# Chunked attention inside a fused block: values per chunk pair, keys spread by masks, shifts moved within SBUF, local matmuls over the column tiles in turn

## The reference

```
x + attn(xn) + ffn(xn)
attn(xn) = (chunk16(xn) + chunk16(every third token of xn)) @ Wo.T + bo     # 16 heads of 8
ffn(xn):  y = xn + mla(rmsnorm(xn, w_ln1));  y + moe(rmsnorm(y, w_ln2))
```

## Time and profile before

| | |
|---|---|
| median of 3 runs | 512.22 us (511.31 to 513.36) |
| the profiled execution, its time | 509.05 us |
| its span (first to last instruction) | 507.3 us |
| busy: PE, DVE, ACT, POOL | 405.5, 315.8, 177.9, 76.7 us |
| mean granted TensorE clock | 0.889 |
| DMA packets | 58215, 24.45 MB; 40088 under 512 B |
| waits of SP's queue | 35.6 us on the shifts' way to DRAM (16 times) |

### The profile page before, as it was taken

How to read it: one execution, slowest core, us unless ns; L and a number is a source line. 1 busy time by engine, 2 the same in 40 slices (tenths; PEclk the granted TensorE clock), 3 DMA queues, 4 the chain that set the end, 5 groups by cost and what they waited for, 6 DMA issues and landing times.

```text
span 507.3 us, 11480 instructions
## 1 busy us (share of the span) xinstructions
PE 405.5 (80%) x4288; PEld 245.2 (48%) x4288; DVE 315.8 (62%) x959; ACT 177.9 (35%) x336; POOL 76.7 (15%) x98
## 2 busy tenths in 40 slices
PE   2753259868497988898978786989989998799995
PEld 2331126554364655455646453645634475464552
DVE  6441037655264777568677565585863288888886
ACT  5143102205152454553334344444564322112110
POOL 6065102240102220304202001000010001000000
PEclk9975659979797999899889987898996899999998
DMA  6052642132181332642232145000400000000000
GB/s 207 0 127 53 118 64 64 15 72 36 25 143 31 71 70 36 105 71 43 44 74 29 26 81 79 7 11 9 121 3 2 1 0 1 23 0 21 1 21 23
DMA packets 58215, 24.45 MB, mean 48 GB/s; under 512 B 40088, under 2 KB 55896, under 8 KB 57368
## 3 DMA queue, kind: packets, MB, share of 16 engines
q1 hardware_dynamic: 58160, 23.71, 24.4%
HBM read 12.94 MB, written 8.55 MB: 42 GB/s over the span
## 4 chain that ended last, share of the span: by engine, by line
PE 25%; DVE 21%; issue 20%; SPq 19%; DMA 8%; POOL 4%; ACT 2%; DVEq 0%; POOLq 0%; ACTq 0%
SPq L541 6%; SPq L556 6%; DVE x L1075 6%; DMA shift_dram<-shift 4%; PE bank_c L1205 4%; DVE k_diag L1055 4%; DVE k_diag L1060 3%; SPq L553 3%; PE bank_B L1294 3%; PE bank_B L1110 3%; SPq L567 3%; PE bank_M L1153 2%; DMA q_stack<-in_c_rows 2%; PE bank_M L1263 2%; PE bank_A L1241 2%
## 5 line engine op out<-in xcount | busy, mean ns | idle before, releaser
L805 ACT ACTIVATE p_mla<-bank_B 128x512 f32<-128x512 f32 (+1 forms) x176 | 95.8, 560 | 130.8 <-PE bank_B L1116 129.8
L934 DVE CUSTOM_DVE_ANT_0 differences<-masks,bank_A 128x512 bf16<-128x512 bf16 (+1 forms) x128 | 78.9, 617 | 67.4 <-PE bank_A L1093 59.1
L1110 PE MATMUL bank_B<-q_stack,k_stack 50*128 50x512 bf16 (+3 forms) x256 | 68.7, 325 | 29.7 <-DMA q_stack<-shift_dram 13.6
L1093 PE MATMUL bank_A<-k_stack,q_stack 50*128 50x512 bf16 (+3 forms) x256 | 66.6, 323 | 16.5 <-DMA q_stack<-in_c_rows 13.9
L1294 PE MATMUL bank_B<-xrT,k_diag 128*128 128x512 f32 x128 | 67.3, 631 | 5.7 <-DVE k_diag L1055 4.5
L1110 PEld LDWEIGHTS bank_B<-q_stack,k_stack 50*128 50x128 bf16 x256 | 20.0, 96 | 76.3 <-issue 47.4
L1263 PE MATMUL bank_M<-v_diag,pT_loc 128*32 128x72 f32 x1088 | 50.6, 238 | 4.7 <-DMA v_diag<-v_dram 4.7
L1205 PE MATMUL bank_c<-p_mla,v_mla 128*9 128x128 f32 (+3 forms) x512 | 51.1, 473 | 3.8 <-ACT p_mla L805 3.3
L1116 PE MATMUL bank_B<-masks 64*128 64x64 bf16 (+1 forms) x512 | 53.6, 211 | 0.0
L1263 PEld LDWEIGHTS bank_M<-v_diag,pT_loc 128*32 128x32 f32 x1088 | 47.5, 113 | 7.6 <-issue 6.0
L1116 PEld LDWEIGHTS bank_B<-masks 64*128 64x128 bf16 x512 | 42.2, 100 | 16.2 <-issue 5.2
(11 more groups left out here) (140 smaller groups left out, 531.7 us busy)
## 6 DMA issues: line engine op xcount, KB each, us to landing
parts_dram<-parts SPq DMA_DIRECT2D x16, 192.0 KB, 2.7
k_stack<-parts_dram SPq DMA_DIRECT2D x8, 384.0 KB
q_stack<-parts_dram SPq DMA_DIRECT2D x8, 384.0 KB
parts_dram<-parts SPq DMA_DIRECT2D x16, 128.0 KB, 2.7
k_diag<-k_part SPq DMA_DIRECT2D x32, 34.0 KB
k_diag<-k_part SPq DMA_DIRECT2D x64, 17.0 KB
x<-in_x SPq DMA_DIRECT2D x4, 256.0 KB, 6.4
parts_dram<-parts SPq DMA_DIRECT2D x16, 64.0 KB, 2.3
```

The lines of the kernel that those rows point to most:

```text
L805: drained_by(nc.scalar.activation(p_of(n)[:, m:m + len(heads), 0:w], src, ACT.Exp, scale=SCALE), step)
L934: drained_by(nc.vector.tensor_tensor_reduce(differences[:, 0:w], masked16[:, S - w:], bank[:, 0:w], -1.0, -NEG, ALU.add, ALU.min, dst), step)
L1093: return nc.tensor.matmul(bank_of(step)[:, n * w:(n + 1) * w], q_stack[b % 2][rows, h % 8, i * P:(i + 1) * P], k_stack[b % 2][rows, h % 8, ...
L1110: nc.tensor.matmul(bank_of(step)[:, m * w:(m + 1) * w], k_stack[b % 2][rows, h % 8, j * P:(j + 1) * P], q_stack[b % 2][rows, h % 8, j * P: ...
```

## The change

Local values: LV makes them per chunk pair, on 32 output partitions each, into three banks (68 records in place of 8), ACT copies them between ones already in `v_rows`, one DMA stores them with those ones, and VD is 2 x 8 DMAs per batch in place of 56. Keys: POOL and ACT write `k_diag` as `k_part` times a mask of a head's rows, 4 pieces of 128 x 1088 each; KD's 24 DMAs per batch go. Shifts: two DMAs within SBUF in place of one to DRAM, a wait and one back. Latent output: Y per group of 4 heads once its `bank_c` is copied, YT and X1 behind the last. LS and LO: the innermost loop goes over the four column tiles. The first stack load (ST 0) stands before the local projections of batch 0, waits for each side's parts by itself, and its rows of ones come first of all; the rows of zeros are no longer loaded. Batch 1's projections, which stood ahead of the first scores, are now strewn between them. `SPREAD` has new numbers: KD of batch 2, for one, stands at S unit 76 of 176 (before: 60), MB of side 1 of batch 2 at 79 (52), ST of batch 2 at 86 (73), and batch 2 begins with unit 88. The last LS of a batch and the first of the next stand at units 21 and 54, 75 and 92, 116 and 130.

```diff
-PT_RING = 2
+PT_RING = 1
+KD_PARTS = 4
+OUTPUT_AT = 3
...
-    "scores": [(-0.289, 3.94)],
+    "scores": [(-0.425, 4.13)],
...
+                if back and k == OUTPUT_AT and n > LEAD:
+                    done = groups[n - LEAD - 1]
+                    found.append([("Y",) + done])
+                    if done[1] == GROUP_ORDER[-1]:
+                        found += [[("YT", done[0])], [("X1", done[0])]]
...
-    steps = first[:1] + first[5:6] + [("WF",)] + first[6:] + first[1:5] + [("KD", 0)]
+    lead = [step for step in first if step == ("XT", 0, 1) or step[0] in ("MA", "MB")]
+    steps = first[:1] + lead[:1] + [("WF",)] + lead[1:] + [("ST", 0)]
+    steps += [step for step in first[1:] if step not in lead] + [("KD", 0, n) for n in range(KD_PARTS)]
...
+        v_rows = sb("v_rows", [P, X, QUADS, VX])
+        v_diag = sb("v_diag", [P, X, 8, QUADS - LOCAL_QUADS, VX])
...
# SP
+                    sp.dma_start(v_dram[b], v_rows[:]).then_inc(v_out, 16)
                 if kind == "VD":
...
+                    if step[2]:
+                        wait_full(sp, ("LO", b, LOCAL_UNITS - 1))
+                    elif b:
+                        wait_full(sp, ("LO", b - 1, NLU - 1))
...
+                    for g in range(X):
+                        sp.dma_start(v_diag[CHUNK * g:CHUNK * g + CHUNK, g, :, 0:i1 - i0, :].rearrange("k q i c -> k q (i c)"),
+                                     v_dram[b, :, g, i0:i1, :].rearrange("(q k) i c -> k q (i c)", k=CHUNK)).then_inc(v_diag_in, 16)
-                if kind == "KD":
...
-                    for h in range(H):
-                        rows = slice(HD * h, HD * h + HD)
-                        if h < X:
-                            sp.dma_start(k_diag[rows, :, h, :], k_part[rows, :, :]).then_inc(k_diag_in, 16)
-                        else:
-                            for par in range(2):
-                                sp.dma_start(k_diag[rows, 1 - par, h - X, :],
-                                             k_part[rows, par, :]).then_inc(k_diag_in, 16)
...
                 if kind == "ST":
-                    sp.wait_ge(parts_out, 16 * 6 * 2 * (b + 1))
...
                     for side in range(2):
+                        sp.wait_ge(parts_out[side], 16 * 6 * (b + 1))
...
                 if kind == "SHIFT":
...
-                    sp.dma_start(shift_dram[b, g].rearrange("r p n -> p r n"), shift[:]).then_inc(shift_out, 16)
-                    sp.wait_ge(shift_out, 16 * (n + 1))
...
-                    sp.dma_start(q_stack[b % 2][row:row + 2, a0:a0 + 4, :],
-                                 shift_dram[b, g].rearrange("r (a i) n -> r a (i n)", i=NT)).then_inc(shift_in[g], 16)
+                    for r in range(2):
+                        sp.dma_start(q_stack[b % 2][row + r:row + r + 1, a0:a0 + 4, :].rearrange("o a (i n) -> o (a i) n", n=P),
+                                     shift[:, r, :]).then_inc(shift_in[g], 16)
...
# POOL (k_part is now sorted in 8 copies of 64 partitions in place of 3 of 128)
+                if step[0] == "KD":
+                    _, b, n = step
...
+                    nc.gpsimd.tensor_scalar(k_diag[:, :, n, :], k_part[:], head_mask[:, n:n + 1], None,
+                                            ALU.mult).then_inc(k_diag_by_pool, 1)
...
# ACT
+                elif kind == "KD":
+                    _, b, n = step
+                    if n == 0:
+                        act.wait_ge(heads_in, 16)
+                        act.wait_ge(k_part_ready, b + 1)
+                        if b:
+                            wait_full(act, ("LS", b - 1, NLU - 1))
+                    x = KD_PARTS + n
+                    nc.scalar.activation(k_diag[:, :, x, :], k_part[:], ACT.Copy,
+                                         scale=head_mask[:, x:x + 1]).then_inc(k_diag_by_act, 1)
...
# PE, LS and LO
-                    for n, pair in enumerate(LUNITS[step[2]][0]):
-                        j, c = n % 4, 2 * P * (n // 4)
+                    pairs = LUNITS[step[2]][0]
+                    for t in range(loc_tiles(step)):
                         for a in range(2):
...
+                            for j, pair in enumerate(pairs[4 * t:4 * t + 4]):
...
-                    for n in range(len(LUNITS[step[2]][0])):
-                        i, j = n // 4, n % 4
+                    for i in range(loc_tiles(step)):
                         for g in range(2):
                             c = 2 * w * i + w * g
                             for par in range(2):
...
+                                for j in range(min(4, len(LUNITS[step[2]][0]) - 4 * i)):
```

More of the change, by code:

```diff
@@ L188, in local @@
     def local(b):
-        steps = [("VD", b, 0), ("VD", b, 1)]
+        steps = [("VD", b, 0)]
         for k in range(NLU + 1):
@@ L193, in local @@
             if k == NLU - 1:
-                steps.append(("KD", b + 1) if b + 1 < B else ("WX",))
+                steps += [("KD", b + 1, n) for n in range(KD_PARTS)] if b + 1 < B else [("WX",)]
             if k:
                 steps.append(("LO", b, k - 1))
-                if k + 1 < NLU:
-                    steps.append(("VD", b, k + 1))
+                if k == LOCAL_UNITS:
+                    steps.append(("VD", b, 1))
             if k < NLU:
@@ L226, in plan @@
     lists.append(([("STATS", 0)], *at["statistics"][0]))
-    return steps + merged(*lists)
+    steps += merged(*lists)
+    at = {step: n for n, step in enumerate(steps)}
+    assert all(at["PICK", b] < at["DOWN", b, 1] and at["X1", b] < at["R2", b] for b in range(B))
+    return steps
 def bank_uses(step):
@@ L468, in loc_tiles @@
             return -(-len(LUNITS[step[2]][0]) // 4)
-        def v_dmas(t):
-            return sum(X * len(LUNITS[k % NLU][1]) for k in range(t % 2, t + 1, 2))
         def wait_full(eng, use):
@@ L524, in _ @@
             for step in steps:
                 kind, b = step[0], step[1] if len(step) > 1 else 0
-                if kind == "LV":
-                    wait_drained(sp, step)
-                    sp.dma_start(v_dram[b, 0:S].rearrange("(i p) d -> p i d", p=P), v_nat).then_inc(v_out, 16)
+                if kind == "LV" and step[2] == (QUADS - 1) // 4:
+                    for n in range(step[2] + 1):
+                        wait_drained(sp, ("LV", b, n))
+                    sp.dma_start(v_dram[b], v_rows[:]).then_inc(v_out, 16)
@@ L529, in _ @@
                 if kind == "VD":
[L530 removed]
+                    i0, i1 = SEGMENTS[step[2]]
                     sp.wait_ge(v_out, 16 * (b + 1))
[L532 to L543 removed]
@@ L567, in _ @@
                             sp.dma_start(parts_dram[b, side, hp, t0:t0 + nt].rearrange("t p n -> p t n"),
-                                         src).then_inc(parts_out, 16)
-                if kind == "ST" and b < 2:
-                    for hp in range(2):
-                        row = SLOT * hp + SHIFT_ROW
-                        sp.dma_start(k_stack[b][row:row + 2, :, :],
-                                     rows_dram[0:2, :].rearrange("o (a n) -> o a n", n=S)).then_inc(k_ones_in[b], 16)
+                                         src).then_inc(parts_out[side], 16)
                 if kind == "ST":
-                    sp.wait_ge(parts_out, 16 * 6 * 2 * (b + 1))
                     if b >= 2:
@@ L721, in _ @@
         def _(act):
-            nc.scalar.memzero(late[:, 0:CLEARED]).then_inc(diag_zeroed, 1)
+            nc.scalar.memzero(v_diag[:].rearrange("p x q i c -> p (x q i c)")).then_inc(v_zeroed, 1)
             act.wait_ge(wide_in, 16)
@@ L1227, in _ @@
                 elif kind == "LV":
-                    for i in range(NT):
-                        last = nc.tensor.matmul(bank[:, i * D:(i + 1) * D].rearrange("p (x g d) -> p x g d", x=X, g=2),
-                                                xnT[:, b % 2, i * P:(i + 1) * P],
+                    for pair in range(16 * step[2], min(16 * step[2] + 16, PAIRS)):
+                        first, stp, n = pair_tokens(pair)
+                        j, c = pair % 4, D * (pair // 4 % 4)
+                        last = nc.tensor.matmul(bank[PAIR * j:PAIR * j + n, c:c + D].rearrange("p (x g d) -> p x g d", x=X, g=2),
+                                                xnT[:, b % 2, first:first + stp * (n - 1) + 1:stp],
                                                 w_attn[:, 2, :].rearrange("p (g x d) -> p x g d", g=2, x=X),
-                                                start=True, stop=True)
+                                                start=True, stop=True, skip_group_check=True)
                     full_by(last, step)
```

262 lines of the change are left out of this document (129 added, 133 removed).

## The result

The changed kernel took **479.38 us** (median of 4, 478.25 to 479.99) against 512.71 for the kernel before on the same chip, a ratio of 0.9351, 95% interval 0.9323 to 0.9378. The forecast was 478. That is so close that one could stop here; the profile shows why one should not.

| | before | after | difference |
|---|---|---|---|
| first maxima matmul | 67.53 | 47.93 | -19.6 |
| from it to the last exponential | 334.9 | 324.7 | -10.2 |
| of that, PE busy | 287.4 | 262.8 | -24.6 |
| of that, PE idle | 47.5 | 61.9 | +14.4 |
| last exponential to the end of the span | 104.9 | 103.8 | -1.1 |

A forecast was written before the change was run, and what follows sets the result against it. Three stages in series: a start waiting for stack loads behind KD's DMAs, scores bound by PE, experts by DVE. Terms sum to -34 us from 509.05: 475 for the profiled execution, 478 for the median, range 456 to 499.

The forecast's parts named there:

- First scores, -19: Start: with KD off SP and ST ahead, stack loads follow the stores and scores start earlier; -19 us, bounds -14 and -21.
- LO, -11: LO over the column tiles in turn: records 27 ns apart, a unit 1.93 us; -11 us, bounds -3 and -25.
- rival 2: More gain than forecast: records run at 15 ns, waits go to their bound, clock stays up; 458 us, chance 0.16.
- Projections of batch 1, +5: Batch 1's projections leave the empty first stage and stand between scores, where PE is short; +5 us, between 0 and +8.
- LV, +3: Local values: 68 records at 27 ns in place of 8, +1 per batch, first hidden; +3 us, bounds +2 and +5.
- Waits of 68 to 157, -14 and +2: Early scores: KD issue, shift waits and VD issues go, -14 us (0 to -19); values' store queues, +2, at most +6.
- KD on ACT and POOL, +1: Mask products: ACT takes them between exponentials (0 to +6 us), POOL's 1.3 us or twice that apiece are covered; +1 us.
- Stacks of batch 2, +3: Before batch 2's scores: stores and loads need 20 us, nine units give 14; +3 us, bounds 0 and +6.
- rival 3: Gain given back: stacks late in two or three batches, ACT's pieces hold exponentials back; 496 us, chance 0.14.
- rival 1: The forecast itself: 478 us, own range 465 to 491, chance 0.62.
- The fourth: Slower: LO, LS and LV matmuls on tiles in turn do not overlap; 573 us, chance 0.04.
- The fifth: Records leave strictly in order, so LS takes 3.4 us a unit now and drops by 2.5; 436 us, chance 0.01.

## Why the prediction was right, and where it was not

The total is right to 1.4 us, but not by its own sum, and that is luck. One group of terms was too small and another had the wrong sign, by about the same amount.

- **First scores, -19:** measured -19.6, by the mechanism given. What the text did not say is that the start's gain reaches the end only if the copies are gone from POOL's and ACT's path as well as from SP's; in the kernel before with early loads 14.7 us became 5.
- **LO, -11:** the step that failed is "I take 27, because LS has the same weights of 128 x 32". The record takes 15.7 ns, rival 2's value, and a unit 1.22 us. The mistake is visible in the rows I had. LS's 27 ns is not a floor of weight loads; it is a fourth of the 107 that a record of 128 columns takes alone, as 15 is a fourth of 60 (both scaled from the 0.43 us of the earlier trace rows, whose weights are 128 columns wide). LV, in turn over the four tiles, has 26 again, (1.08 - 0.27) / 31. All three stand at a fourth of their own length. That the number of tiles sets the fourth shows in the last unit of a batch, whose 2 pairs use two tiles (lines below): 50 ns for LS and 29 for LO, a half. The term was 13.6 us of PE and came out at 27.4. What it shortens the end by is 11 to 15 in the changed kernel, and about 19 where the waits are gone.
- **LS, 0:** right. 1.12 us a unit before and 1.08 after, and its old order is not slower.
- **Projections of batch 1, +5, and LV, +3:** all PE work but LO's and LS's in the window rose by 4.3 us, 262.8 - 23.2 - 22.3 against 287.4 - 50.6 - 23.8; +8 was given.
- **Waits of 68 to 157, -14 and +2:** wrong in sign. PE stood 19.4 us there; in the stretch that answers to it (48 to 134) it stood 86 - 60.3 = 25.7. Nor did the 3 us for the clock come: granted were 0.82 and 0.81, where it was 0.82 and 0.91. The waits named in the earlier trace rows did go: those for shifts, and `v_diag` is down to 0.4. In their place came 3.1 us for POOL's `q_part`, 8.6 for POOL's split by way of DVE, and 6.7 for batch 1's stacks.
- **KD on ACT and POOL, +1:** failed, in two ways. The piece on POOL costs 3.04 us, above both ends (1.3 and twice that). And the sentence "it is covered" looked only at who waits for `k_diag`, not at what POOL does next: the split of the parts stands behind the last product, and DVE and PE behind the split. The queries stand behind the products too, and LS waited 4.8 us for them. The run with short products prices it all at 13 us.
- **Stacks of batch 2, +3:** the mechanism is right, the size was 8.7; and batch 1's stacks, of which nothing was said, are late by 6.7. The runs with all products on ACT put that down to the place of the projections and to the third shift ahead of the loads on SP. The two numbers for the projections take 9 us away.
- **Y and the tail, -2:** -1.1, with 103.8 us after the last exponential (103 was given). In DVE's timeline an expert's step is the 2.97 us between these two:

```profile
433.65 1.13 DVE L1088 SCALAR_TENSOR_TENSOR x<-bank_A,expert_w,x 128x128 f32<-128x128 f32 x4 [0.21 <-DVE k_diag L1073]
436.62 1.13 DVE L1088 SCALAR_TENSOR_TENSOR x<-bank_A,expert_w,x 128x128 f32<-128x128 f32 x4 [0.21 <-DVE k_diag L1073]
```

So the forecast ran like this. Between first scores and last exponential it gave -13 (the sum less first scores and tail), and -10.2 came. Of it, PE's work was about -6 (+5, +3 and LO's -13.6) and came out at -24.6; its idle time was about -7 and came out at +14.4. Of its own tests, one failed as written: "if PE stands still for more than 50 us between first scores and last exponential", and it stood 61.9. It is rival 2 and rival 3 together, whose effects happen to be as large as one another, under the number of rival 1.

**The other rivals.** The fourth (tiles in turn don't overlap) is out with 15.7 ns a record. The fifth (strict order) is out too: LS's unit did not move. Its 3.4 us for LS were also too high by its own rule, which lets a tile's first record run beside the last one of the tile before: 8 x 3 x 0.107 + 0.107 = 2.7. The 1.12 excludes that as well. It speaks against order and waiting on the same tile together, and does not tell which of the two fails.

The page's price for LO (TensorE: Matmul & The Clock Gate, "LDWEIGHTS", of the Trainium skill: 27 ns for 32 columns) is not borne out for loads that go to the column tiles in turn. The trace has LO's 64 weight loads of a unit in 1.04 us, 16 ns each:

```profile
69.45 1.04 PEld L1282 LDWEIGHTS bank_M<-v_diag,pT_loc 128*32 128x32 f32 x64
```

And the last units of a batch, LS with 8 records on two tiles, (0.62 - 0.27) / 7 = 50 ns each, and LO with 16, (0.67 - 0.23) / 15 = 29, in PE's timeline:

```profile
84.04 0.62 PE L1259 MATMUL bank_A<-k_diag,q_part 128*32 128x128 f32 x8
189.76 0.67 PE L1282 MATMUL bank_M<-v_diag,pT_loc 128*32 128x72 f32 x16
```

## What to carry to other kernels

Before a row is used as a floor, put it beside the record's own length: two shapes at the same fraction of it are under one limit, and it scales. When work moves to an engine that had room, price what stands behind it in that engine's order, not only who wants its result. And when a forecast comes out right, check it term by term: behind the right total stood some 26 us of waits, won by moving four products per batch to ACT and by three numbers of the order.

## What was not expected of the hardware

- A product of 1088 float32 columns with a per-partition scalar takes POOL 3.04 us and ACT 1.20 us. With the 32 columns in 0.363 us that is (3.04 - 0.363) / 1056 = 2.5 ns a column on POOL, more than its product of two tensors, at most 1.15 / 512 = 2.25. The Trainium skill (GPSIMD Engine Reference, "4.1 Engine selection") calls operations with one input roughly line-rate on GpSimd; this one is not.
- Matmuls of 32 stationary columns take a fourth of their estimated single length per record when the four column tiles come in turn (two records of one matmul, then the next tile), down to 15.7 ns, weights loaded with each, and a half with two tiles. With four records in a row on one tile (LS) the same fourth is reached, with eight (LO before) only 40 ns of 60. Whether eight in a row set the 40, or that two matmuls in a row add into the same place, no run separates.
- In the kernel before, the new loops lowered the granted clock of the scores from 0.89 to 0.84; in the changed kernel, with new or old loops, it was 0.90 and 0.92. That the clock fell because PE waited more is my reading; no run separates the two.
